# Self-attention over pixels on Trainium2: halves of the first image, the order of GpSimd's queue, and the last store

## The chip, the core and the metric

The kernel runs on one core of a Trainium2 (trn2) chip. The metric is the device time of one execution in microseconds (us); lower is better. Before the change the median of 3 runs is 163.97 us (163.97 to 164.14).

## The reference

For each of 4 images with 256 channels and 32x32 = 1024 pixels, in float32:

```python
q = einsum('oc,bcn->bon', Wq, xf) + bq      # 32 x 1024
k = einsum('oc,bcn->bon', Wk, xf) + bk      # 32 x 1024
v = einsum('oc,bcn->bon', Wv, xf) + bv      # 256 x 1024
attn = softmax(einsum('bqi,bqj->bij', q, k), axis=-1)
out = einsum('bcj,bij->bci', v, attn) + xf
```

## The kernel before, in words

**Numbers in two parts.** TensorE multiplies in the type fp32r. Each operand is cut into a high part (a cast) and a low part (the rest after the cast), and a product is three matmuls: high by high, high by low, low by high. So x, the weights, q, k, v and the exponentials all have a cast and a subtraction somewhere. `x_hi`, `x_lo`, `v_hi`, `v_lo`, `w_hi`, `w_lo` are these parts; the cast is mostly ScalarE's or VectorE's, the subtraction VectorE's or GpSimd's.

**Stages of an image.** (1) q and k are projected, 512 pixels at a time (`project_qk`, for image 0 `first_project_qk`). For images 1 to 3 their parts go by DMA into two stacks of 96 rows, `q_a` and `k_a` (helper `blocks`, L236), so that one matmul does the three products. (2) Score groups t = 0 to 7 of 128 query pixels by 1024 keys go to PSUM; VectorE takes the negative row maximum (L653), ScalarE the exponentials' sum (L492). Maximum and log of the sum are the shift of a row. (3) The shifts are turned into rows by a transpose (L692), split in two and sent by DMA as rows 96 and 97 of `q_b` (`send_rows`, L256). (4) The scores are made again, transposed, keys by queries, with the shift as two more rows of the contraction: the tiles `st` of L981, 16 an image, n = 16 b + 8 h + j, h being the half of the query pixels and j the block of 128 keys. ScalarE's exponential of a tile is then a finished softmax weight (L527 its high part, L530 in full); L400 or L720 make the low part. (5) `weigh_v` adds v times the weights into `acc`, three matmuls for each of two channel tiles (L994 twice, L1000 once). (6) VectorE adds x and the bias (`finish`), and SyncE stores.

**Image 0's first half is different.** Its sums aren't waited for: the shift of its 512 first query pixels is the maximum alone (`first_shifts`, `first_rows`, `put_first_rows`), and the result is divided afterwards. VectorE inverts the four sums of each partition (L667), SyncE writes them to a row in DRAM (`inv_row`, L312) and reads the row back on all partitions (`inv_all`, L316). At the end of that half VectorE multiplies `acc` by `inv_all` into `scaled` (L746), and GpSimd adds it to x (L467), to which ScalarE has added the bias (L506).

**The order of the work** is written out by hand. `turn(b)` has 16 steps; in step s TensorE makes the tile st of n + 2, weighs tile n, and then does the piece of the next image's front that `FRONT` (L44) gives to the step: score groups, q and k, v. Each other engine has a `turn` of its own, and waits on semaphores only. The order inside an engine's queue is thus what decides who is behind whom: GpSimd's loop (L451) comes at n = 8, 24 and 40 to the blocks of the next image's first half, to the shift rows of this image's second half, and to the blocks of the second half. `send_rows` waits until the rows are turned and, for b > 0, until the tiles that still read the old rows are done. The tile n = 8 (16 b + 8 in general) waits for `row_in[1]` of both rows, for `q_b` and for the exponential of tile n - 1.

```python
if j == 0:
    if b == 0 and h == 0:
        pe.wait_ge(row_put, 1)
    ...
    else:
        pe.wait_ge(row_in[h], rows_in(b, h))
    pe.wait_ge(qb_in[h], DMA * (b + 1))
```

**The start.** SyncE loads image 0 in two transfers, one for each tile of 128 channels (L275), then Wv (L276) and image 1 (L279). ScalarE loads the small weights (L473), which VectorE splits (L610, L612). x is cast and split in four pieces, `piece(i)`: channel tile i // 2, pixel half i % 2. TensorE goes through the same four (L861, L864, L866); the two halves of q and k are complete after pieces 2 and 3 (`qk_ready`). Then ScalarE makes k high (L542, both halves), the second quarter of q high (L548) and q in full for the second half (L553); VectorE makes the first quarter of q high (L754), q low (L634) and k low (L628); GpSimd copies q high (L372) behind the low part of Wv (L422). TensorE meanwhile does v tiles 0 and 1, then the score groups 0, 1, 2.

**The end.** The last image's second half lies in separate banks. `weigh_last_block` finishes channel tile 0, then the third and the fourth quarter of channel tile 1; `finish_last` (L729) evicts each quarter, and ScalarE's queue (L596) and SyncE's (L353) store them.

Of the kernel before, what the change touches and what calls it, by code (L numbers as in the profile page):

```python
# [6 lines left out]
def nonlocal_attention(nc, x, small, wv_t, out):  # L7
# [52 lines left out]
    with ctx:  # L60
# [3 lines left out]
        def sem(name):  # L64
            return ctx.enter_context(nc.semaphore(name))
# [36 lines left out]
        scaled = sb("scaled", [P, CT, HALF])  # L102
# [9 lines left out]
        x0_in = [sem(f"x0_in{c}") for c in range(CT)]  # L112
# [66 lines left out]
        x0_biased = sem("x0_biased")  # L179
        first_half_made = sem("first_half_made")  # L180
# [11 lines left out]
        def piece(i):  # L192

            return i // 2, cols(i % 2)
# [78 lines left out]
        def _(sp):  # L273
            for c in range(CT):
                sp.dma_start(x_sb[:, 0, c, :], x_v[0, :, c, :]).then_inc(x0_in[c], DMA)  # L275
# [35 lines left out]
            with nc.allow_non_contiguous_dma("512 numbers, long ahead of their use"):  # L311
                sp.dma_start(inv_row.rearrange("(t p) -> p t", p=P), inv[:, :]).then_inc(inv_put, DMA)  # L312
# [43 lines left out]
            sp.wait_ge(quarter_sent, DMA)  # L356

        @block.gpsimd
        def _(pool):
# [91 lines left out]
            for n in range(TH, TILES):  # L451
                b, more = n // PER, n // PER + 1 < BATCH
                if n % PER == JT:
                    if more:
                        second_blocks(b + 1, 0)
                    send_rows(pool, b, 1, (HI, LO) if more else (LO,))
                    if more:
                        second_blocks(b + 1, 1)
                split_w(n)
                if n == PER:  # L460

                    pool.wait_ge(w_split_pool, SPLIT_COUNT[n])
                    pool.wait_ge(st_ready, PER + 5)
                    pool.wait_ge(x0_biased, CT)
                    for c in range(CT):
                        pool.wait_ge(acc_read, c + 1)
                        nc.gpsimd.tensor_tensor(x_sb[:, 0, c, cols(0)], scaled[:, c, :], x_sb[:, 0, c, cols(0)],  # L467
                                                ALU.add).then_inc(first_half_made, 1)
                        pool.wait_ge(first_half_made, c + 1)

        @block.scalar
        def _(act):
            act.dma_start(small_sb[:, :], small).then_inc(small_in, DMA)  # L473
            act.preload_act_table_set("natural_log_exp_and_others")
            for i in range(4):
                c, part = piece(i)
                act.wait_ge(x0_in[c], DMA)
# [67 lines left out]
            def put_q_hi():  # L545

                act.wait_ge(q_lo_put, 1)
                nc.scalar.activation(q_a[2 * CQK:3 * CQK, Q_PARTS[1]], q_home(1),  # L548
# [10 lines left out]
            put_k_hi(0)  # L559
            put_k_hi(1)  # L560
            put_q_hi()
# [587 lines left out]
```

## Time and profile before

| | |
|---|---|
| median of 3 runs | 163.97 us (163.97 to 164.14) |
| profiled execution | 164.95 us |
| its span, first to last instruction | 163.2 us |
| mean granted TensorE clock | 0.998 of full speed |
| TensorE busy | 157.8 us (97%), 788 matmuls |
| VectorE busy | 133.3 us (82%) |
| ScalarE busy | 109.2 us (67%) |
| GpSimd busy | 57.3 us (35%) |
| DMA | 14.67 MB, mean 90 GB/s |

The profile is one execution; times within it are counted from its first instruction. PE is TensorE, DVE VectorE, ACT ScalarE, POOL GpSimd, SP SyncE; a q behind the name means its DMA queue. "x2" after an instruction means that two of them follow each other and are shown as one row with their time together. L981 is line 981 of the kernel. In brackets stands the idle time of the engine ahead of a row and who ended it. Instructions of one engine overlap a little at their ends, so two in a row take less than twice one.

### The profile page before, as it was taken

How to read it: one execution, taken by the hardware profiler on the slowest of the kernel's cores; microseconds unless marked ns; L12 is line 12 of the kernel's file. 1: busy time of each engine (PE TensorE's matmuls, PEld its weight loads, DVE VectorE, ACT ScalarE, POOL GpSimd, SP SyncE). 2: the span in 40 equal slices, each digit the busy share in tenths (PEclk: the TensorE clock that was granted, in tenths of full speed). 3: DMA queues.
4: the chain of work that ended last, by engine and by line, in shares of the span. 5: the costliest groups of instructions: out<-in, count | busy, mean ns of one | idle time of the engine just before them, and what ended most of it. 6: DMA issues, size and time to landing. Idle time of an engine off the chain costs nothing.

```text
span 163.2 us, 2451 instructions
## 1 busy us (share of the span) xinstructions
PE 157.8 (97%) x788; PEld 132.4 (81%) x788; DVE 133.3 (82%) x214; ACT 109.2 (67%) x200; POOL 57.3 (35%) x66
## 2 busy tenths in 40 slices
PE   7999999989999999999999999999999999999992
PEld 5677888778888898798888898789888898788882
DVE  1899998875988989996999989895989679846951
ACT  3679887958999647746999655745896655756400
POOL 4479945434243304733343300342433300124500
PEclk9999999999999999999999999999999999999999
DMA  4576796591002130246310230152220330003003
GB/s 157 190 296 177 229 46 27 151 290 51 25 30 60 37 129 2 57 108 209 129 48 18 83 129 2 33 135 78 96 84 1 96 129 0 0 5 129 0 0 129
DMA packets 8020, 14.67 MB, mean 90 GB/s; under 512 B 1872, under 2 KB 2312, under 8 KB 8008
## 3 DMA queue, kind: packets, MB, share of 16 engines
q1 hardware_dynamic: 7112, 13.52, 30.8%
q0 software_dynamic: 608, 0.80, 2.0%
q10 hardware_dynamic: 288, 0.20, 0.4%
q8 instruction: 6, 0.10, 0.4%
q14 instruction: 6, 0.05, 0.1%
HBM read 4.79 MB, written 4.20 MB: 55 GB/s over the span
## 4 chain that ended last, share of the span: by engine, by line
PE 90%; DMA 2%; ACT 2%; DVE 2%; issue 2%
PE acc L994 32%; PE acc L1000 16%; PE slot L834 11%; PE st L981 9%; PE slot L894 7%; PE slot L994 5%; DMA small_sb<-small 2%; PE slot L1000 2%; ACT dump L492 2%; PE slot L846 2%; PE slot L851 2%; PE slot L920 1%; DVE negmax L653 1%; PE slot L866 1%; DVE x_lo L618 0%
## 5 line engine op out<-in xcount | busy, mean ns | idle before, releaser
L400 POOL TENSOR_TENSOR w_lo<-w_full,w_hi 128x512 fp32r<-128x512 f32 x21 | 28.1, 1336 | 54.7 <-ACT w_full L530 31.0
L994 PE MATMUL acc<-w_hi,v_hi 128*128 128x512 f32 x112 | 44.3, 396 | 0.0
L994 PE MATMUL acc<-w_hi,v_lo 128*128 128x512 f32 x112 | 44.1, 394 | 0.0
L530 ACT ACTIVATE w_full<-st 128x512 f32<-128x512 f32 x62 | 36.8, 593 | 7.6 <-PE st L981 7.5
L492 ACT ACTIVATE dump<-slot,negmax 128x1024 f32<-128x1024 f32 x29 | 32.4, 1119 | 9.9 <-DVE negmax L653 9.5
L653 DVE TENSOR_REDUCE negmax<-slot 128x1 f32<-128x1024 f32 x29 | 35.2, 1216 | 3.8 <-PE slot L894 3.8
L1000 PE MATMUL acc<-w_lo,v_hi 128*128 128x512 f32 x112 | 37.4, 396 | 0.0
L720 DVE TENSOR_TENSOR w_lo<-w_full,w_hi 128x512 fp32r<-128x512 f32 x43 | 31.6, 740 | 3.3
L981 PE MATMUL st<-q_b,k_b 98*128 98x512 f32 x62 | 24.6, 399 | 0.9 <-issue 0.8
L994 PEld LDWEIGHTS acc<-w_hi,v_hi 128*128 128x128 f32 x112 | 21.1, 189 | 5.0 <-issue 0.3
L994 PEld LDWEIGHTS acc<-w_hi,v_lo 128*128 128x128 f32 x112 | 21.2, 189 | 4.8
L1000 PEld LDWEIGHTS acc<-w_lo,v_hi 128*128 128x128 f32 x112 | 21.0, 188 | 4.8
L711 DVE CAST w_hi<-w_full 128x512 fp32r<-128x512 f32 x40 | 18.0, 453 | 3.1 <-ACT w_full L530 1.5
L527 ACT ACTIVATE w_hi<-st 128x512 fp32r<-128x512 f32 x24 | 14.3, 595 | 7.1 <-PE st L981 7.1
L834 PE MATMUL slot<-wv_hi,x_hi 128*128 128x256 f32 x62 | 17.4, 281 | 0.4 <-ACT dump L492 0.4
L834 PE MATMUL slot<-wv_lo,x_hi 128*128 128x256 f32 x62 | 17.4, 280 | 0.0
L834 PE MATMUL slot<-wv_hi,x_lo 128*128 128x256 f32 x62 | 17.3, 280 | 0.0
L894 PE MATMUL slot<-k_a,q_a 96*128 96x512 f32 x48 | 15.2, 397 | 0.0
L519 ACT ACTIVATE v_hi<-slot 128x512 fp32r<-128x512 f32 x12 | 7.2, 599 | 11.8 <-PE slot L834 11.8
L701 DVE TENSOR_TENSOR v_lo<-slot,v_hi 128x512 fp32r<-128x512 f32 x16 | 11.0, 690 | 4.4 <-ACT v_hi L519 4.2
L894 PEld LDWEIGHTS slot<-k_a,q_a 96*128 96x128 f32 x48 | 13.0, 310 | 1.1
L981 PEld LDWEIGHTS st<-q_b,k_b 98*128 98x128 f32 x62 | 11.6, 188 | 2.4 <-issue 1.0
(101 smaller groups left out, 214.9 us busy)
## 6 DMA issues: line engine op xcount, KB each, us to landing
out<-x_sb SPq DMA_DIRECT2D x7, 512.0 KB, 2.8
x_sb<-x SPq DMA_DIRECT2D x3, 1024.0 KB, 6.3
k_b<-k_a SPq DMA_DIRECT2D x8, 192.0 KB, 2.6
q_b<-q_a SPq DMA_DIRECT2D x8, 192.0 KB, 2.6
x_sb<-x SPq DMA_DIRECT2D x2, 512.0 KB, 4.2
k_a<-qk_parts SPq DMA_DIRECT2D x12, 64.0 KB, 2.3
q_a<-qk_parts SPq DMA_DIRECT2D x12, 64.0 KB, 2.3
k_a<-qk_parts POOLq DMA_DIRECT2D x6, 64.0 KB, 2.6
```

The lines of the kernel that those rows point to most:

```text
L400: nc.gpsimd.tensor_tensor(w_lo[:, r, :], w_full[:, r, :], w_hi[:, r, :].bitcast(fp32), ALU.subtract).then_inc(w_split_pool, 1)
L492: nc.scalar.activation(dump[:, t % 2, :], s_home(b, t), ACT.Exp, bias=negmax[:, t:t + 1], accum_out=rowsum[:, t:t + 1]).then_inc(rowsum_re ...
L527: nc.scalar.activation(w_hi[:, r, :], st_home(n), ACT.Exp).then_inc(w_cut_act, 1)
L530: nc.scalar.activation(w_full[:, r, :], st_home(n), ACT.Exp).then_inc(exp_done, 1)
L653: nc.vector.tensor_reduce(out=negmax[:, t:t + 1], in_=s_home(b, t), op=ALU.max, axis=AX.X, negate=True).then_inc(negmax_ready, 1)
L711: nc.vector.tensor_copy(w_hi[:, r, :], w_full[:, r, :]).then_inc(w_cut_dve, 1)
L720: nc.vector.tensor_tensor(w_lo[:, r, :], w_full[:, r, :], w_hi[:, r, :].bitcast(fp32), ALU.subtract).then_inc(w_split_dve, 1)
L834: last = nc.tensor.matmul(dst, lhs, rhs, start=(i == 0), stop=(i == len(terms) - 1))
L894: last = nc.tensor.matmul(s_home(b, t)[:, cols(h)], pixels(b, t), k_a[0:K_A, cols(h)], start=True, stop=True)
L981: nc.tensor.matmul(st_home(n), k_b[0:K_B, j * P:(j + 1) * P], q_b[0:K_B, cols(h)], start=True, stop=True).then_inc(st_ready, 1)
L994: nc.tensor.matmul(dst, v[:, b % 2, j, c * P:(c + 1) * P], w_hi[:, n % RING, part], start=(j == 0 and v is v_hi), stop=False)
L1000: return nc.tensor.matmul(dst, v_hi[:, b % 2, j, c * P:(c + 1) * P], w_lo[:, n % RING, part], start=False, stop=(j == JT - 1))
```

## The change

1. Image 0 is loaded in two transfers by pixel halves (each with both channel tiles, rows of 2 KB and not 4 KB), and cast, split and projected in that order.
2. ScalarE makes the first quarter of q high too, between the two halves of k high; VectorE begins with k low.
3. TensorE makes score group 0 ahead of v tile 1.
4. `inv_row` keeps the order in which the sums lie in SBUF, so a partition writes 16 bytes in one piece; the readers undo the order.
5. VectorE copies `acc` of image 0's first half and doesn't multiply; GpSimd multiplies it by `inv_all` after step n = 16 and adds it to x at n = 24, ahead of its subtraction for tile 24.
6. GpSimd sends the shift rows ahead of the blocks of the next image's first half.
7. The last quarter is evicted in two pieces of 128 columns, stored by SyncE and by ScalarE's queue.

```diff
-                sp.dma_start(x_sb[:, 0, c, :], x_v[0, :, c, :]).then_inc(x0_in[c], DMA)
+                sp.dma_start(x_sb[:, 0, :, cols(h)], x_v[0, :, :, cols(h)]).then_inc(x0_in[h], DMA)
...
         def piece(i):
-            return i // 2, cols(i % 2)
+            return i % CT, cols(i // CT)
...
+        LAST_PIECES = ((slice(0, QUARTER),), (slice(QUARTER, QUARTER + P), slice(QUARTER + P, HALF)))
...
-                sp.dma_start(inv_row.rearrange("(t p) -> p t", p=P), inv[:, :]).then_inc(inv_put, DMA)
+            sp.dma_start(inv_row.rearrange("(p t) -> p t", p=P), inv[:, :]).then_inc(inv_put, DMA)
...
             sp.wait_ge(acc_read, 4 * BATCH + 1)
-            sp.dma_start(out_v[BATCH - 1, :, 1, quarter(3)], x_sb[:, BATCH - 1, 1, quarter(3)]).then_inc(out_sent[1], DMA)
+            sp.dma_start(out_v[BATCH - 1, :, 1, N - QUARTER:N - P], x_sb[:, BATCH - 1, 1, N - QUARTER:N - P]).then_inc(out_sent[1], DMA)
...
                 if n % PER == JT:
-                    if more:
-                        second_blocks(b + 1, 0)
                     send_rows(pool, b, 1, (HI, LO) if more else (LO,))
                     if more:
-                        second_blocks(b + 1, 1)
+                        for h in range(2):
+                            second_blocks(b + 1, h)
+                if n == PER + JT:
+                    pool.wait_ge(st_ready, n + 1)
+                    pool.wait_ge(x0_biased, CT)
+                    for c in range(CT):
+                        nc.gpsimd.tensor_tensor(x_sb[:, 0, c, cols(0)], undivided[:, c, :], x_sb[:, 0, c, cols(0)],
+                                                ALU.add).then_inc(first_half_made, 1)
+                    pool.wait_ge(first_half_made, CT)
                 split_w(n)
                 if n == PER:
                     pool.wait_ge(w_split_pool, SPLIT_COUNT[n])
-                    pool.wait_ge(st_ready, PER + 5)
-                    pool.wait_ge(x0_biased, CT)
+                    pool.wait_ge(inv_in, DMA)
                     for c in range(CT):
                         pool.wait_ge(acc_read, c + 1)
-                        nc.gpsimd.tensor_tensor(x_sb[:, 0, c, cols(0)], scaled[:, c, :], x_sb[:, 0, c, cols(0)],
-                                                ALU.add).then_inc(first_half_made, 1)
-                        pool.wait_ge(first_half_made, c + 1)
+                        pool.wait_ge(w_split_dve, SPLIT_COUNT[PER + AHEAD + c])
+                        nc.gpsimd.tensor_tensor(undivided[:, c, :].rearrange("p (t q) -> p t q", t=TH),
+                                                undivided[:, c, :].rearrange("p (t q) -> p t q", t=TH),
+                                                inv_all[:, :].rearrange("p (q t) -> p t q", t=TH),
+                                                ALU.mult).then_inc(first_half_divided, 1)
+                    pool.wait_ge(first_half_divided, CT)
...
             put_k_hi(0)
+            put_q_hi(0)
             put_k_hi(1)
-            put_q_hi()
+            put_q_hi(1)
             put_q2_full()
...
+            act.wait_ge(acc_read, 4 * BATCH + 2)
+            act.dma_start(out_v[BATCH - 1, :, 1, N - P:N], x_sb[:, BATCH - 1, 1, N - P:N]).then_inc(quarter_sent, DMA)
...
                 if (b, h) == (0, 0):
-                    dve.wait_ge(inv_in, DMA)
-                    nc.vector.tensor_tensor(scaled[:, c, :], acc[:, c, :], inv_all[:, :],
-                                            ALU.mult).then_inc(acc_read, 1)
+                    nc.vector.tensor_copy(undivided[:, c, :], acc[:, c, :]).then_inc(acc_read, 1)
                     return
...
-            dve.wait_ge(qk_ready, 1)
-            nc.vector.tensor_scalar(out=q_a[2 * CQK:3 * CQK, Q_PARTS[0]], in0=q_home(0),
-                                    scalar1=bias[2 * CQK:3 * CQK, 0:1], scalar2=None,
-                                    op0=ALU.add).then_inc(q_hi_put, 1)
+            put_k_lo(0)
             put_q_lo(0)
-            put_k_lo(0)
             put_k_lo(1)
             put_q_lo(1)
...
-                dst = qk_home(0, i % 2)
+                dst = qk_home(0, i // CT)
...
             v_tile(0, 0)
+            first_scores(0)
             v_tile(0, 1)
-            first_scores(0)
             first_scores(1)
             first_scores(2)
```

## Rows read from the trace of the kernel before

**Rows 1.** Stretch 36.6 to 160.3 us: busy of each engine (instructions), TensorE clock, DMA.
```profile
36.60:160.30 123.70, 123.69 (x612) 105.22 (x612) 102.93 (x165) 82.08 (x152) 35.29 (x34) 1.00 0.21 65
```

**Rows 2.** Chain of waits, start: start us, us, what.
```profile
0.76 3.94 DMA small_sb<-small
...
5.47 0.71 DVE x_lo L618
...
8.57 0.23 PE slot L866
```

**Rows 3.** TensorE in order of time, 35 to 75 us: start us, us, instruction.
```profile
35.50 0.28 PE L834 MATMUL slot<-wv_hi,x_lo 128*128 128x256 f32 x1
36.57 0.47 PE L981 MATMUL st<-q_b,k_b 98*128 98x512 f32 x1 [0.79 <-issue]
...
38.29 0.63 PE L894 MATMUL slot<-k_a,q_a 96*128 96x512 f32 x2
...
73.95 0.28 PE L834 MATMUL slot<-wv_hi,x_lo 128*128 128x256 f32 x1
74.07 0.40 PE L981 MATMUL st<-q_b,k_b 98*128 98x512 f32 x1
```

**Rows 4.** VectorE, GpSimd and SyncE's queue in order of time, 30 to 35 us.
```profile
30.24 0.41 DVE L692 STREAM_TRANSPOSE shift_rows<-shift_parts 128x128 f32<-128x128 f32 x1
...
30.82 0.65 POOL L237 DMA_DIRECT2D k_a<-qk_parts  x1 [2.45 <-ACT qk_parts L485]
...
31.96 1.16 POOL L262 DMA_DIRECT2D q_b<-shift_rows  x2
...
34.53 0.59 SPq L237 DMA_DIRECT2D k_a<-qk_parts  x1
```

**Rows 5.** DMA issues: KB each, us to landing; all, then from 17, then from 31.9.
```profile
x_sb<-x SPq DMA_DIRECT2D x3, 1024.0 KB, 6.3
...
out<-x_sb SPq DMA_DIRECT2D x1, 128.0 KB, 1.9
...
q_b<-shift_rows POOLq DMA_DIRECT2D x7, 2.0 KB, 2.4
...
x_sb<-x SPq DMA_DIRECT2D x1, 1024.0 KB, 13.6
inv_row<-inv SPq DMA_DIRECT2D x1, 2.0 KB, 10.5
...
q_b<-shift_rows POOLq DMA_DIRECT2D x2, 2.0 KB, 4.0
```

**Rows 6.** DMA queues, 3.2 to 3.7 us: packets, MB, share of 16 engines.
```profile
q1 hardware_dynamic: 42, 0.17, 83.5%
q10 hardware_dynamic: 43, 0.02, 15.0%
```

**Rows 7.** ScalarE, VectorE and TensorE in order of time, 4 to 15 us.
```profile
4.51 1.15 ACT L478 ACTIVATE x_hi<-x_sb 128x512 fp32r<-128x512 f32 x2 [2.04 <-DMA x_sb<-x]
...
8.21 1.31 ACT L542 ACTIVATE k_a<-slot,small_sb 64x512 fp32r<-64x512 f32 x2 [0.70 <-PE slot L866]
...
9.18 1.40 DVE L628 SCALAR_TENSOR_TENSOR k_a<-slot,small_sb,k_a 32x512 fp32r<-32x512 f32 x2
...
13.68 0.73 PE L920 MATMUL acc<-k_a,q_a 96*128 96x512 f32 x2
...
14.57 1.21 DVE L653 TENSOR_REDUCE negmax<-acc 128x1 f32<-128x1024 f32 x1
```

**Rows 8.** GpSimd, then TensorE in order of time, 63 to 79 us.
```profile
63.35 2.78 POOL L467 TENSOR_TENSOR x_sb<-scaled,x_sb 128x512 f32<-128x512 f32 x2 [7.92 <-PE st L981]
...
78.96 0.39 PE L1000 MATMUL acc<-w_lo,v_hi 128*128 128x512 f32 x1
```

**Rows 9.** VectorE in order of time, the last evictions.
```profile
157.48 0.75 DVE L750 SCALAR_TENSOR_TENSOR x_sb<-slot,small_sb,x_sb 128x512 f32<-128x512 f32 x1 [0.94 <-PE slot L1000]
...
160.33 0.48 DVE L729 SCALAR_TENSOR_TENSOR x_sb<-slot,small_sb,x_sb 128x256 f32<-128x256 f32 x1 [0.94 <-PE slot L1000]
```

More of the change, by code:

```diff
@@ L110, in nonlocal_attention @@
         slot = [ctx.enter_context(nc.psum_tensor(f"slot{i}", [P, N], fp32)) for i in range(2)]
-        x0_in = [sem(f"x0_in{c}") for c in range(CT)]
+        x0_in = [sem(f"x0_in{h}") for h in range(2)]
         x1_in = sem("x1_in")
@@ L179, in nonlocal_attention @@
         x0_biased = sem("x0_biased")
+        first_half_divided = sem("first_half_divided")
         first_half_made = sem("first_half_made")
@@ L310, in _ @@
             sp.wait_ge(inv_ready, 1)
-            with nc.allow_non_contiguous_dma("512 numbers, long ahead of their use"):
-                sp.dma_start(inv_row.rearrange("(t p) -> p t", p=P), inv[:, :]).then_inc(inv_put, DMA)
+            sp.dma_start(inv_row.rearrange("(p t) -> p t", p=P), inv[:, :]).then_inc(inv_put, DMA)
             sp.wait_ge(x_in, DMA)
@@ L453, in _ @@
                 if n % PER == JT:
-                    if more:
-                        second_blocks(b + 1, 0)
                     send_rows(pool, b, 1, (HI, LO) if more else (LO,))
                     if more:
-                        second_blocks(b + 1, 1)
+                        for h in range(2):
+                            second_blocks(b + 1, h)
[6 more added lines that the diff above has]
+                    pool.wait_ge(first_half_made, CT)
                 split_w(n)
@@ L476, in _ @@
                 c, part = piece(i)
-                act.wait_ge(x0_in[c], DMA)
+                act.wait_ge(x0_in[i // CT], DMA)
                 nc.scalar.activation(x_hi[:, 0, c, part], x_sb[:, 0, c, part], ACT.Copy).then_inc(x0_cut, 1)
@@ L723, in finish_last @@
             def finish_last(i):
-                part = slice(HALF + i * QUARTER, HALF + (i + 1) * QUARTER)
                 if i == 0:
@@ L728, in finish_last @@
                     dve.wait_ge(av_done, TILES)
-                nc.vector.scalar_tensor_tensor(
-                    out=x_sb[:, BATCH - 1, 1, part], in0=last_half(1)[i][1],
-                    scalar=bv_sb[:, 1:2], in1=x_sb[:, BATCH - 1, 1, part],
-                    op0=ALU.add, op1=ALU.add).then_inc(acc_read, 1)
+                for px in LAST_PIECES[i]:
+                    part = slice(HALF + px.start, HALF + px.stop)
+                    nc.vector.scalar_tensor_tensor(
+                        out=x_sb[:, BATCH - 1, 1, part],
+                        in0=last_half(1)[i][1][:, px.start - i * QUARTER:px.stop - i * QUARTER],
+                        scalar=bv_sb[:, 1:2], in1=x_sb[:, BATCH - 1, 1, part],
+                        op0=ALU.add, op1=ALU.add).then_inc(acc_read, 1)
             def finish(b, h, c):
```

12 lines of the change are left out of this document (6 added, 6 removed).

## The prediction

> **What bounds the kernel now.** I read the stretches first, then the chain of waits, then each engine in order of time. From 36.6 to 160.3 us TensorE is busy 123.69 of 123.70 us at the full granted clock, the upper of its two levels (2.4 GHz) [rows 1]. In that stretch no work on another engine can shorten the run; it can only lengthen it, by being late for a matmul. Three places are left: the start, one hole near 36 us, and the last eviction and store.
>
> The start's chain runs from the small weights, which land 3.94 us after their issue, over VectorE's first split of x at 5.47 and TensorE's projection, whose last matmul begins at 8.57 [rows 2], to the splits of q and k, the first row maxima and the exponentials. The hole [rows 3]: image 1's v projection starts its last matmul at 35.50, and the next instruction, the score tile n = 8, starts at 36.57, 0.79 us of that idle with no releaser named. At the same place of image 2 the two stand at 73.95 and 74.07. The distance is 1.07 us against 0.12, and the tile behind the wait takes 0.47 us and not 0.40. So the hole costs 0.95 + 0.07 = 1.02 us.
>
> Who is late? That tile waits for the two transfers of shift rows. Their numbers are ready at 30.24 + 0.41 = 30.65, but GpSimd issues two q, k blocks first (from 30.82) and the two rows only from 31.96, for 1.16 us together, the second so at about 32.54 [rows 4]. They need 4.0 us to land, where 2.4 is the median of such rows [rows 5]: 32.54 + 4.0 = 36.54, and the tile starts at 36.57. They are slow because the queues are full: x of image 3, issued beside inv_row, took 13.6 us, where 6.3 is the median of three such images, and inv_row, 2 KB in pieces of 4 bytes, took 10.5 us [rows 5].
>
> **The change, part by part.**
>
> *The hole.* Two edits meet. inv_row is written in 128 pieces of 16 bytes, no longer 512 of 4. If the cost goes by piece, 10.5 us becomes 2 + 8.5/4, about 4 us (2 for a landing that waits for nothing, as the last store's 1.9 [rows 5]); image 3 and the broadcast of inv behind it land before 30 us, and the blocks and rows meet idle queues. And GpSimd sends the rows ahead of its blocks, at 30.7 and 31.3. Landing in 2.4 us, the second is there at 33.7, 1.9 us before TensorE would ask at 35.62. If the queues stay full, 4.0 us give 35.3, and as what is issued sooner waits longer for the same queue I leave 0.4 us of wait. Term -1.02; ends -0.6 and -1.02. I take the upper end, since image 2 landed twice as fast without inv_row beside it. The Trainium skill, page "DMA: Bandwidth & Descriptors", section "Specifications", says that below 512 B the engine does a read-modify-write; pieces of 16 bytes remain below, so that would leave a cost for each of the 128, and the same term.
>
> Moved past: GpSimd's four blocks end their issue when they did, as only their order with the rows changes and the last two wait for the second half's cut. Of SP's own blocks the last one that image 1's first scores need is issued at 34.53 [rows 4]. With the start's gain (below) that is 34.15, landed with 2.4 us at 36.55; the scores, now at 38.29 [rows 3], would come at 38.29 - 1.40 = 36.89. The cover is 0.3 us; price 0, at worst 0.4.
>
> *The start.* Pieces 0 and 1 are now the two channel tiles of the first 512 pixels. The first half of q and k is complete three matmuls of 0.23 us (0.70) sooner, the second half no sooner, at 8.80 [rows 2]. ScalarE casts k high 0, q high 0, k high 1. Its two k casts now run from 8.21 for 1.31 us, to 9.52 [rows 7]: k high 1 is bound by the second half's 8.80 and still ends there, and q high 0 fits in front of it. VectorE loses q high 0. Its two k low splits end at 9.18 + 1.40 = 10.58 now [rows 7]; with k low 0 done long before, k low 1 takes 0.74 us (half of the 1.40 and a start of its own) from 9.55, to 10.29. So the first maximum comes 0.29 us sooner. But score group 0 now stands ahead of v tile 1 (6 matmuls, 0.70 us), which then delays groups 1 to 3: group 3 starts at about 13.75 (13.68 now), takes 0.73, so the fourth maximum, now at 14.57, starts at 14.4 [rows 7]. Of 0.29 us 0.18 are left at the shift rows, for which TensorE waits next.
>
> Beyond this, x arrives in rows of 2 KB. From 3.2 to 3.7 us 42 rows of q1 (x, 4 KB) went beside 43 of q10 (the small weights), one for one. A row of q1 takes 0.835 x 16 x 0.5 / 42 = 0.159 us of an engine, one of q10 0.028 us [rows 6]. The eight small rows of an engine so take 8 x 0.187 = 1.5 us; beside x rows of half the size 8 x 0.108 = 0.9, 0.6 us less. Not all of it counts: x's first cast starts at 4.51 [rows 7] and takes some 0.6, so the first split, at 5.47 now, can gain 0.34 at most. For twice the rows of x I allow 0.14 back. So 0.20 more. Term for the start: -(0.18 + 0.20) = -0.38; ends 0 and -0.55.
>
> The Trainium skill, page "DMA: Bandwidth & Descriptors", section "Queues, rings and completion order", says that an engine drains a packet of about 9 to 17 descriptors from one queue before it turns to the next. The trace's one for one does not look like that; by the rule x's row size would not matter here, and this term would be -0.18.
>
> *The first half of image 0.* VectorE copies acc and no longer multiplies it, the same 128x512 read of PSUM, at a place where TensorE is never late: 0. GpSimd takes over the multiplication, two operations more, in the gap before 63.35 where it sat idle for 7.92 us [rows 8]: 0. Its two additions move to behind the tile n = 24, which starts at 74.07 [rows 3], and hold back GpSimd's w_lo of n = 24: tile done 74.47, additions 2.78 us as now, 77.3, then w_lo (as one addition, 1.39) 78.7. TensorE uses it at 78.96 [rows 8]. Cover 0.3 us; price 0, at worst 0.15 if each of the three ran 0.14 slower. SP's store of that half waits for the additions; what is queued behind it waits for image 1's eviction at the same place anyway: 0.
>
> *The end.* The last eviction of 256 columns becomes two of 128. 512 columns took 0.75 us and 256 took 0.48 [rows 9], so 128 take about 0.35; started 0.25 apart, they end 0.12 later than now. The second store moves 64 KB where one moved 128 KB in 1.9 us [rows 5]; I allow 0.07 for the smaller size. Term +0.05; ends -0.1 and +0.15.
>
> **Sum.** -1.02 - 0.38 + 0.05 = -1.35 us. The profiled execution took 164.95 us (span 163.2, 1.75 around it) and would take 163.60. The median, 163.97, lies 0.98 below the profiled one; I carry the difference over: 162.62. About 0.2% (0.33 us) is what a measurement of this kernel can tell from no change.
>
> **The rivals.**
> 1. *The small weights land as before*, by the page's packets or because halves of x cost what is won. The start gives 0.18, the sum is -1.15: 162.8 us. For it: no row prices x in 2 KB rows at this moment. Chance 0.20.
> 2. *The queues stay full*: inv_row costs by the transfer, not by the piece, and only the new order helps. -0.6 - 0.38 + 0.05: 163.0 us. For it: no 16-byte piece is in the trace. Chance 0.10.
> 3. *A cover of 0.3 us fails*, that of w_lo 24 or of the last k block, by 0.3 to 0.4: 163.0 us. The Trainium skill, page "SBUF — State Buffer", section "Who interferes with whom", says that a VectorE instruction with two SBUF inputs contends with GpSimd's reads. The 1.39 us an addition is a row beside a busy VectorE. Chance 0.13.
> 4. *The change doesn't do what it is for*: the hole has another cause and stays. -0.38 + 0.05: 163.64 us, the edge of no change. Against it: 36.54 and 36.57 agree. Chance 0.07.
> 5. *Slower*: GpSimd's multiplication reads inv with a stride of four numbers, which no row shows, and the shift rows of image 1's second half stand behind it in its queue. They must be issued by 71 us to be in at 74; the multiplications begin near 61.3, so it decides from some 4.5 us each. At 6 us each the rows land near 77 and TensorE waits 2.9 us: 165.5 us. Against: that is over four times an addition. Chance 0.04.
>
> **Numbers.** The forecast keeps 0.46. Range 162.1 to 163.5: below, the start's 0.55 and a shorter tail, and 0.2 for the carrying over; above, rivals 1 to 3 with the upper end of the tail and one of the covers. Faster by over 0.2%: forecast and rivals 1 to 3, 0.89, less 0.02 for several at once; within 0.2%: rival 4 and near misses, 0.08; slower 0.05.
>
> **What the next profile would show.** Right: no idle time ahead of the tile behind image 1's v projection; inv_row lands in 3 to 5 us and image 3 in 6 to 8; the small weights are used near 4.2; k low 1 ends 0.3 to 0.5 sooner; the additions run from 74.5 less the gain, and w_lo 24 is in time. Wrong: a new TensorE gap at image 1's first scores or at its n = 8, or multiplications of over 3 us on GpSimd, or 4.7 us again for the small weights.

## The result: no gain, and the profile after

In 14 executions each, the changed kernel took 164.22 us (median; 164.03 to 164.43) and the kernel before 163.94 us (163.79 to 164.29). The ratio is 1.0015, with a 95% interval of 1.0008 to 1.0022: slower by 0.15%, inside the 0.2% that the prediction called no change. 162.6 us was forecast, with a range of 162.1 to 163.5. The profiled execution took 164.22 us (span 162.4). Below, "before" and "after" without an article mean the profiled executions of the two kernels, and the name of an experiment its profiled execution where a time within it is given.

The stretch from the end of the old hole to the last evictions, as in [rows 1]: TensorE is busy at the full granted clock, and the hole in front of it is gone (second fence, in order of time; the answer to [rows 3]).

```profile
36.10:159.60 123.50, 123.48 (x613) 105.06 (x611) 103.67 (x166) 82.58 (x153) 38.01 (x36) 1.00 0.21 67
```

```profile
35.90 0.28 PE L847 MATMUL slot<-wv_hi,x_lo 128*128 128x256 f32 x1
36.02 0.40 PE L994 MATMUL st<-q_b,k_b 98*128 98x512 f32 x1
```

The two starts lie 0.12 us apart, where there were 1.07. But the last matmul of the v projection, which started at 35.50, now starts at 35.90. The transfers [rows 5] did what the forecast said, and more; the DMA issues from 0 to 60 us (KB each, us to landing):

```profile
x_sb<-x SPq DMA_DIRECT2D x2, 512.0 KB, 4.7
...
q_b<-shift_rows POOLq DMA_DIRECT2D x2, 2.0 KB, 1.7
...
inv_row<-inv SPq DMA_DIRECT2D x1, 2.0 KB, 2.1
```

inv_row lands in 2.1 us and not 10.5, the shift rows in 1.7 and not 4.0. The 0.4 us by which the v projection is late are lost at the start. ScalarE, then VectorE, then GpSimd in order of time (the answer to [rows 7]):

```profile
4.98 1.15 ACT L490 ACTIVATE x_hi<-x_sb 128x512 fp32r<-128x512 f32 x2 [2.50 <-DMA x_sb<-x]
6.40 1.15 ACT L490 ACTIVATE x_hi<-x_sb 128x512 fp32r<-128x512 f32 x2 [0.27 <-DMA x_sb<-x]
7.45 0.61 ACT L570 ACTIVATE wv_hi<-wv 128x512 fp32r<-128x512 f32 x1
7.97 0.67 ACT L554 ACTIVATE k_a<-slot,small_sb 64x512 fp32r<-64x512 f32 x1
8.67 0.47 ACT L561 ACTIVATE q_a<-slot,small_sb 32x256 fp32r<-32x256 f32 x1
9.16 0.68 ACT L554 ACTIVATE k_a<-slot,small_sb 64x512 fp32r<-64x512 f32 x1
```

```profile
3.79 0.29 DVE L626 CAST wqk_hi<-small_sb 128x256 fp32r<-128x256 f32 x1 [2.51 <-DMA small_sb<-small]
...
8.68 0.74 DVE L644 SCALAR_TENSOR_TENSOR k_a<-slot,small_sb,k_a 32x512 fp32r<-32x512 f32 x1 [0.32 <-ACT k_a L554]
9.45 0.48 DVE L650 SCALAR_TENSOR_TENSOR q_a<-slot,small_sb,q_a 32x256 fp32r<-32x256 f32 x1
9.96 0.74 DVE L644 SCALAR_TENSOR_TENSOR k_a<-slot,small_sb,k_a 32x512 fp32r<-32x512 f32 x1
...
14.81 1.23 DVE L669 TENSOR_REDUCE negmax<-acc 128x1 f32<-128x1024 f32 x1
16.15 0.38 DVE L676 CAST shift_parts<-negmax 128x4 fp32r<-128x4 f32 x1
```

```profile
15.89 0.61 POOL L408 CAST x_hi<-x_sb 128x512 fp32r<-128x512 f32 x1
16.58 1.31 POOL L412 TENSOR_TENSOR x_lo<-x_sb,x_hi 128x512 fp32r<-128x512 f32 x1
```

The first cast of x starts 0.47 us later than before (4.51), k low 1 ends at 10.70 (10.58), and the fourth maximum starts at 14.81 (14.57). VectorE's cast of the shifts takes 0.38 us and ends with GpSimd's cast beside it: 15.89 + 0.61 = 16.50, 16.15 + 0.38 = 16.53. Before, VectorE and GpSimd:

```profile
15.89 0.20 DVE L660 CAST shift_parts<-negmax 128x4 fp32r<-128x4 f32 x1
16.13 0.17 DVE L662 TENSOR_TENSOR shift_parts<-negmax,shift_parts 128x4 fp32r<-128x4 f32 x1
...
20.72 2.35 DVE L653 TENSOR_REDUCE negmax<-slot 128x1 f32<-128x1024 f32 x2
```

```profile
15.45 0.61 POOL L406 CAST x_hi<-x_sb 128x512 fp32r<-128x512 f32 x1
```

The image's first half and the end, the answers to [rows 8] (GpSimd) and [rows 9] (VectorE):

```profile
60.74 1.54 POOL L477 TENSOR_TENSOR undivided<-undivided,inv_all 128x512 f32<-128x512 f32 x1 [6.00 <-DVE w_lo L736]
63.86 1.55 POOL L477 TENSOR_TENSOR undivided<-undivided,inv_all 128x512 f32<-128x512 f32 x1 [1.58 <-DVE w_lo L736]
...
73.87 2.54 POOL L466 TENSOR_TENSOR x_sb<-undivided,x_sb 128x512 f32<-128x512 f32 x2 [2.73 <-PE st L994]
76.49 2.54 POOL L402 TENSOR_TENSOR w_lo<-w_full,w_hi 128x512 fp32r<-128x512 f32 x2
```

```profile
159.62 0.61 DVE L747 SCALAR_TENSOR_TENSOR x_sb<-slot,small_sb,x_sb 128x128 f32<-128x128 f32 x2 [0.94 <-PE slot L1013]
```

### The profile page after: what moved, and what is told of

Same layout as the page of the kernel before. It is cut to its first block, busy times and chain, and to the rows that moved or that the text cites. A ratio compares the mean times of both kernels' runs of the same rounds, so it can differ in the third digit from the quotient of the medians.

```text
span 162.4 us, 2456 instructions
## 1 busy us (share of the span) xinstructions
PE 157.1 (97%) x788; PEld 131.9 (81%) x788; DVE 133.8 (82%) x214; ACT 109.6 (67%) x201; POOL 59.2 (36%) x68
## 4 chain that ended last, share of the span: by engine, by line
PE 90%; DMA 3%; ACT 2%; DVE 1%; issue 1%; SPq 0%; DVEq 0%
PE acc L1007 32%; PE acc L1013 16%; PE slot L847 13%; PE st L994 9%; PE slot L907 7%; PE slot L1007 5%; DMA x_sb<-x 3%; PE slot L1013 2%; PE slot L859 2%; PE slot L864 2%; PE slot L933 1%; DVE k_a L644 1%; ACT dump L504 1%; ACT x_hi L490 1%; ACT k_a L554 0%
## 5 line engine op out<-in xcount | busy, mean ns | idle before, releaser
L736 DVE TENSOR_TENSOR w_lo<-w_full,w_hi 128x512 fp32r<-128x512 f32 x43 | 30.7, 719 | 3.3
L727 DVE CAST w_hi<-w_full 128x512 fp32r<-128x512 f32 x40 | 19.5, 490 | 3.0 <-ACT w_full L542 1.4
L265 POOL DMA_DIRECT2D q_b<-shift_rows x7 | 4.2, 602 | 29.5 <-DVE shift_rows L708 27.0
```

Of the source, the lines that this page charges most:

```text
L727: nc.vector.tensor_copy(w_hi[:, r, :], w_full[:, r, :]).then_inc(w_cut_dve, 1)
L736: nc.vector.tensor_tensor(w_lo[:, r, :], w_full[:, r, :], w_hi[:, r, :].bitcast(fp32), ALU.subtract).then_inc(w_split_dve, 1)
```

## The experiments

Each kernel was timed in five rounds beside the kernel before on the same chip. "Ratio" is to that kernel; its own median stands in the last column, since it moved from chip to chip. A median is that of 12 or 13 executions, but of 6 for rest_alone and rest_beside and of 5 for four_back.

| kernel | median us (range) | ratio, 95% | before there |
|---|---|---|---|
| before_again | 164.19 (163.84 to 165.09) | 0.9989, 0.9972 to 1.0007 | 164.45 |
| start_alone | 164.92 (164.28 to 165.31) | 1.0024, 1.0007 to 1.0041 | 164.45 |
| rest_alone | 163.82 (163.73 to 164.10) | 0.9962, 0.9943 to 0.9981 | 164.45 |
| load_alone | 164.61 (164.09 to 165.78) | 1.0014, 0.9991 to 1.0036 | 164.45 |
| whole | 164.32 (164.15 to 164.49) | 1.0002, 0.9990 to 1.0014 | 164.28 |
| order_back | 164.23 (164.05 to 164.40) | 0.9998, 0.9987 to 1.0009 | 164.28 |
| inv16_alone | 164.52 (164.40 to 164.87) | 1.0018, 1.0005 to 1.0030 | 164.28 |
| rows_first_alone | 164.01 (163.88 to 164.74) | 0.9989, 0.9975 to 1.0003 | 164.28 |
| tiles_4k | 164.22 (164.11 to 164.33) | 0.9987, 0.9973 to 1.0001 | 164.32 |
| rows_2k | 164.29 (164.03 to 164.95) | 1.0001, 0.9987 to 1.0016 | 164.32 |
| rest_again | 163.89 (163.75 to 164.18) | 0.9971, 0.9956 to 0.9987 | 164.32 |
| rest_old_end | 163.92 (163.82 to 164.09) | 0.9975, 0.9964 to 0.9986 | 164.32 |
| four_loads | 164.21 (163.75 to 164.39) | 0.9982, 0.9967 to 0.9997 | 164.40 |
| four_back | 163.89 (163.70 to 163.93) | 0.9966, 0.9954 to 0.9978 | 164.40 |
| rest_beside | 163.81 (163.73 to 164.12) | 0.9965, 0.9952 to 0.9978 | 164.40 |
| four_clear | 164.67 (164.18 to 164.99) | 1.0008, 0.9995 to 1.0022 | 164.43 |
| whole_clear | 164.91 (164.82 to 166.71) | 1.0022, 1.0009 to 1.0035 | 164.43 |
| rest_clear | 164.67 (164.52 to 164.92) | 1.0010, 0.9995 to 1.0026 | 164.43 |

### The change cut in two: before_again, start_alone, rest_alone, load_alone

before_again is the kernel before with nothing changed, for a second look at its hole. start_alone is that kernel with items 1 to 3 of the change (the loads, ScalarE's q, the score group), rest_alone the changed kernel without them, so items 4 to 7. load_alone is the kernel before with item 1 alone:

```diff
-            for c in range(CT):
-                sp.dma_start(x_sb[:, 0, c, :], x_v[0, :, c, :]).then_inc(x0_in[c], DMA)
+            for h in range(2):
+                sp.dma_start(x_sb[:, 0, :, cols(h)], x_v[0, :, :, cols(h)]).then_inc(x0_in[h], DMA)
...
-            return i // 2, cols(i % 2)
+            return i % CT, cols(i // CT)
...
-                dst = qk_home(0, i % 2)
+                dst = qk_home(0, i // CT)
```

Expected of before_again:

> The kernel before, unchanged, for another profiled execution. Theory A (the hole near 36 us belonged to one execution, not to the kernel): span near 162.2 us, no idle time ahead of the score tile behind image 1's v projection, time within 0.1% of the kernel before. Theory B (the hole is in every execution and the change filled it, but lost as much elsewhere): span near 163.2 us with 0.7 us or more of idle time at that place.

Expected of start_alone:

> The kernel before with the start's edits alone (x of image 0 by halves, ScalarE makes q high's first quarter, score group 0 ahead of v tile 1). Theory A: all of the loss is here and a little more, since the last store gains: +0.3 to +0.5 us against the kernel before. Theory B (the loss comes from GpSimd's new work or its order): 0 to +0.1 us, or the 0.38 us less that were forecast.

Expected of rest_alone:

> The changed kernel with the start as in the kernel before; it keeps inv_row by 16 bytes, the rows ahead of the blocks, GpSimd's multiplication and the last store in two pieces. Theory A (no hole in most executions, the last store gains a little): -0.05 to -0.2 us against the kernel before. Theory B (GpSimd's part loses): +0.2 us or more. If the hole were in every execution of the kernel before: -1.0 us.

Expected of load_alone:

> The kernel before with only the load, the cast and the projection of image 0 by halves; q high's first quarter stays with VectorE, the score groups keep their place. Theory A1 (x lands about 0.4 us later because the small weights' rows now pass ahead of x, and this is what costs): x's first cast near 5.0 us and not 4.5, +0.2 to +0.4 us. Theory A2 (the order of score group 0 and v tile 1 is what costs): 0 us or a gain.

The two parts pull against each other: items 4 to 7 win (0.9962), items 1 to 3 lose (1.0024). Item 1 alone is unclear in its median (1.0014, with 1 inside the interval). And before_again showed what no single trace could. TensorE in order of time in its profile:

```profile
35.48 0.28 PE L834 MATMUL slot<-wv_hi,x_lo 128*128 128x256 f32 x1
35.81 0.47 PE L981 MATMUL st<-q_b,k_b 98*128 98x512 f32 x1
```

In the same kernel the two starts lie 0.33 us apart here, where [rows 3] has 1.07 and a matmul without a hole 0.12. In start_alone and load_alone, which keep the old rest, it is 36.95 - 35.86 = 1.09 and 36.29 - 35.91 = 0.38: a hole of another length each time. These three kernels are spread over 1.0 to 1.7 us, rest_alone over 0.37. The hole explains the profiled times to 0.05 us. Counted as the prediction counts it, it cost 1.02 us in before, 0.28 in before_again and 0.69 in rows_2k (below), whose transfers were those of the kernel before. Without it 163.93, 163.88 and 163.89 us are left of the 164.95, 164.16 and 164.58.

### Which edit closes the hole: inv16_alone, rows_first_alone

inv16_alone is the kernel before with inv_row in pieces of 16 bytes; VectorE's multiplication (L746) undoes the order. rows_first_alone is the kernel before with item 6 alone.

```diff
...
-                sp.dma_start(inv_row.rearrange("(t p) -> p t", p=P), inv[:, :]).then_inc(inv_put, DMA)
+            sp.dma_start(inv_row.rearrange("(p t) -> p t", p=P), inv[:, :]).then_inc(inv_put, DMA)
...
```

```diff
-                    if more:
-                        second_blocks(b + 1, 0)
                     send_rows(pool, b, 1, (HI, LO) if more else (LO,))
                     if more:
-                        second_blocks(b + 1, 1)
+                        for h in range(2):
+                            second_blocks(b + 1, h)
```

> The kernel before with inv_row in pieces of 16 bytes alone; VectorE's multiplication reads inv_all with a stride. Theory A: inv_row lands in about 2 us, the hole is gone, the spread of the times is under 0.5 us, the median 163.8 to 163.95 us. Theory D (the order of GpSimd's queue fills the hole, not the queues' load): the hole stays at 0.3 us or more.

> The kernel before with the shift rows ahead of the blocks on GpSimd alone. Theory A (the queues are full until image 3 and the broadcast have landed, whatever is issued first): the rows are issued 1.1 us sooner and land 0.3 to 1.1 us sooner, the hole shrinks but the spread stays near 1 us. Theory D: the hole is gone and so is the spread.

Either closes it in its profile. inv16_alone, TensorE, and the transfer of image 3 from 15 to 40 us; then the same two of rows_first_alone:

```profile
35.88 0.28 PE L835 MATMUL slot<-wv_hi,x_lo 128*128 128x256 f32 x1
35.99 0.40 PE L982 MATMUL st<-q_b,k_b 98*128 98x512 f32 x1
...
x_sb<-x SPq DMA_DIRECT2D x1, 1024.0 KB, 5.3
```

```profile
35.63 0.28 PE L833 MATMUL slot<-wv_hi,x_lo 128*128 128x256 f32 x1
35.75 0.40 PE L980 MATMUL st<-q_b,k_b 98*128 98x512 f32 x1
...
x_sb<-x SPq DMA_DIRECT2D x1, 1024.0 KB, 12.8
```

With 16-byte pieces image 3 lands in 5.3 us; with 4-byte pieces it still takes 12.8, and the rows, sent first, are in time all the same, but not by much. They need 3.1 us here, the second from about 32.2 on, so they are in at 35.3 for a tile at 35.75; the 4.0 us of [rows 5] would be too late (an estimate from these rows). The times say so too: rows_first_alone is spread over 0.86 us, with 3 of its 12 executions at 164.25, 164.54 and 164.74, inv16_alone over 0.47. So the order by itself closes the hole in most executions, as far as the times show, and not in all. inv16_alone isn't faster for it, because VectorE's strided multiplication costs more than the hole. VectorE, first there and then in before_again:

```profile
39.44 2.06 DVE L745 TENSOR_TENSOR scaled<-acc,inv_all 128x512 f32<-128x512 f32 x2
```

```profile
39.33 1.28 DVE L746 TENSOR_TENSOR scaled<-acc,inv_all 128x512 f32<-128x512 f32 x2
```

TensorE's score tile behind the two starts at 42.84 and not 42.21, where it was 0.08 late ahead of them: 0.55 us. GpSimd's strided multiplications (1.54 and 1.55 us above) stand where nobody waits for them, so item 5 is what makes item 4 pay.

### Why the start loses: whole, order_back, tiles_4k, four_loads, four_back

whole is the changed kernel again, a second look with its start in the same series. The other four are the changed kernel with one thing each: order_back puts v tile 1 ahead of score group 0 again; tiles_4k loads by channel tile again, in rows of 4 KB, and keeps the order of the pieces; four_loads loads image 0 in four transfers of 256 KB in the order of the pieces; four_back is four_loads with order_back's edit.

```diff
-            for h in range(2):
-                sp.dma_start(x_sb[:, 0, :, cols(h)], x_v[0, :, :, cols(h)]).then_inc(x0_in[h], DMA)
+            for i in range(4):
+                c, part = piece(i)
+                sp.dma_start(x_sb[:, 0, c, part], x_v[0, :, c, part]).then_inc(x0_in[i], DMA)
...
```

> The changed kernel, unchanged, on the chip on which the kernel before is timed beside it. Theory A (the hole near 36 us is there in every execution but of changing length, 0.3 to 1.1 us, since inv_row's slow write lands at changing times): the times lie within 0.5 us of each other, where those of the kernel before spread over 1 us or more; the median is 0.3 to 0.6 us above the kernel without the start's edits (163.82 us), so at 164.1 to 164.4.

> The changed kernel with v tile 1 again ahead of score group 0. Theory A (x's late landing costs 0.2 us and more, the order of the score group the rest): 0.1 to 0.2 us below the whole change, and the fourth maximum starts 1.13 us after the third. Theory C (the order is neutral, the loss is all x's landing): the same time as the whole change.

> The changed kernel, projected by halves, but image 0 loaded by channel tile in rows of 4 KB as before, so that piece 1 waits for the second transfer. Theory E: x's first cast is back at 4.5 us and the last at 6.9 us; since piece 1 now starts with the second transfer, TensorE ends its projections near 8.8 us, as in the whole change: 164.1 to 164.4 us, 0.3 us or more above the kernel without the start's edits.

> The changed kernel with image 0 in four transfers of 256 KB, a quarter for each piece, in the order of the pieces; the rows stay at 2 KB. Theory G (only the landing of the halves is late; the new order of the start is worth the 0.2 to 0.3 us that were forecast once x is there in time): first cast at 4.5 us or sooner, first maximum 0.2 us or more sooner than in the kernel before, 0.3 to 0.6 us less than the whole change: 163.7 to 164.0 us. Theory H (the new order is worth nothing, since VectorE's three steps and ScalarE's three casts follow each other without cover and v tile 1 delays the groups behind): the first cast is in time, the time stays at 164.1 us or above.

> The same with v tile 1 ahead of score group 0 again. Theory G: 0.1 us below the one with the new place, as for the whole change (164.32 against 164.23 us), so 163.6 to 163.9 us. Theory H: 164.0 us or above.

First the load. x's first cast starts at 4.46 to 4.66 us in every kernel that loads by channel tile, tiles_4k (4.59) among them, and at 4.97 to 5.28 in every one that loads by halves. The queues from 3.2 to 3.7 us (packets, MB, share of 16 engines); start_alone, then whole:

```profile
q1 hardware_dynamic: 53, 0.11, 77.9%
q10 hardware_dynamic: 50, 0.03, 18.9%
```

```profile
q1 hardware_dynamic: 70, 0.14, 90.8%
q10 hardware_dynamic: 11, 0.00, 2.2%
```

A row of 2 KB takes 0.779 x 8 / 53 = 0.118 us or 0.908 x 8 / 70 = 0.104 us of an engine here, and not half of the 0.159 us of a row of 4 KB [rows 6]. By these two the first 512 KB, 256 such rows, need 1.66 to 1.89 us of 16 engines, where 128 of the old ones took 1.27: 0.4 to 0.6 us more (an estimate). The small weights do land sooner in whole and after, 3.0 us after their issue, and are used at 3.8, as the forecast had it, but x is late by then and nothing is won. In start_alone, order_back and tiles_4k they need 3.9 to 4.0. So in some executions the weights' rows pass x's one for one, in others not. rows_2k, the kernel before with each row of x written as two, was meant to price the row by itself, but its rows went out joined again (as many packets on q1 as before). The same 2 KB rows, 4 KB apart too, took less in the kernels with four transfers: in the same half microsecond 80 of them went by in four_back at 89.2%, which is 0.089 us each, and 96 in four_clear at 91.4%, 0.076. So neither the size nor the distance alone makes them dear; what does stays open.

Nor is late x the whole loss. tiles_4k has x's first cast in time and is no faster than whole: 164.22 us, 0.33 above rest_again beside it. Its piece 1 needs the second channel tile and so waits for the second transfer; its last cast of x ends at 5.90 + 1.67 = 7.57, that of after at 6.40 + 1.15 = 7.55.

> The kernel before with image 0 still loaded by channel tile, but each row of 4 KB written as two pieces of 2 KB. Theory E (a row of 2 KB costs the queue more than half a row of 4 KB, at the start of the stream above all): twice the rows of x in the queue's count, x's first cast near 4.9 us and not 4.5, the time 0.2 to 0.4 us above the kernel before. Theory F (the late landing has to do with the two halves lying 4 KB apart, not with the size of a row): x's first cast near 4.5 us.

Then the order of the work. v tile 1's place changes little in the halves kernel (order_back, 164.23 against 164.32). Between four_loads and four_back lie 0.32 us (164.21 and 163.89), but that this is the order isn't shown. The two load x alike, and yet TensorE's last projection matmul starts 0.77 us apart in their profiles; four_loads, then four_back:

```profile
8.54 0.39 PE L880 MATMUL slot<-x_lo,wqk_hi 128*128 128x512 f32 x1
```

```profile
7.77 0.48 PE L880 MATMUL slot<-x_lo,wqk_hi 128*128 128x512 f32 x1
```

In four_clear, which loads as four_back does and has its order, it is 8.37. So the landing of four transfers moves from execution to execution, and four_back's median is that of five. Its profile has everything of the forecast's start: the first cast at 3.85, the last projection matmul at 7.77 and not 8.41, the fourth maximum at 14.20. Still the last matmul of image 1's v projection starts at 35.41 us, in rest_beside at 35.55, in the kernel before at 35.50. In VectorE's and GpSimd's order of time, four_back:

```profile
14.20 1.22 DVE L670 TENSOR_REDUCE negmax<-acc 128x1 f32<-128x1024 f32 x1
15.52 0.48 DVE L677 CAST shift_parts<-negmax 128x4 fp32r<-128x4 f32 x1
16.04 0.17 DVE L679 TENSOR_TENSOR shift_parts<-negmax,shift_parts 128x4 fp32r<-128x4 f32 x1
...
20.63 2.35 DVE L670 TENSOR_REDUCE negmax<-slot 128x1 f32<-128x1024 f32 x2
```

```profile
15.37 0.61 POOL L409 CAST x_hi<-x_sb 128x512 fp32r<-128x512 f32 x1
```

The cast of 128x4 numbers begins 0.37 us earlier than in the kernel before (15.89) and ends 0.09 earlier, at 16.00, 0.02 after GpSimd's 15.98. In before it ended at 16.09 (GpSimd 16.06), in start_alone at 16.47 (16.44), in after at 16.53 (16.50), in whole at 16.57 (16.54). That is a gate nobody wrote: GpSimd's second cast of image 1, whose place follows from ScalarE's q in full for the second half, over GpSimd's copies and splits of q. In before that q ends at 10.58, in after at 11.00, and GpSimd's work behind it is 0.42 to 0.44 us later. The Trainium skill, page "SBUF — State Buffer", section "Who interferes with whom", says that a VectorE copy or cast in its two-port mode and a GpSimd instruction exclude each other for the whole instruction. The common ends agree with it; the last three kernels try it. Common ends alone prove little: in load_alone the maxima are so late (the fourth at 15.02) that the cast takes 0.17 us, and it still ends 0.04 after GpSimd's.

What the end of this cast decides can be read from VectorE. From the subtraction behind it VectorE works without a pause up to image 1's first row maximum, which starts 4.59 us later in before (20.72 - 16.13) and in four_back (20.63 - 16.04), and 4.59 to 4.60 later in all 17 profiles in which GpSimd's queue is not edited as below. The last matmul of image 1's v projection starts 19.37 to 19.43 us after the cast's end in the same 17. four_back's first score tiles do start 0.29 us before those of before (17.39 and 17.68), but at 23.84 and 23.93 only 0.09 of it is left. So TensorE gains at 35 us what the cast of the shifts gains at 16, and no more.

### The gate taken away: four_clear, whole_clear, rest_clear

four_back, the changed kernel, and rest_alone, each with this edit of GpSimd's queue:

```diff
+            pool.wait_ge(shift_ready, 1)
             cut_x1(1)
             split_x1(1)
             pool.wait_ge(x1_split, 2)
-            pool.wait_ge(shift_ready, 1)
             cut_x1(2)
             split_x1(2)
             pool.wait_ge(x1_split, 3)
-            cut_x1(3)
-            pool.wait_ge(x1_cut, 4)
             split_w(1)
+            cut_x1(3)
+            pool.wait_ge(x1_cut, 4)
```

> The kernel four_back (image 0 in four transfers, v tile 1 ahead of score group 0, everything else as in the change), and in GpSimd's queue its second cast of image 1 (L408) waits until the first shifts are split (shift_ready), while the fourth cast goes behind the subtraction for tile 1. So no cast of GpSimd runs beside VectorE's cast of the shifts. Theory 'the shift cast is held by GpSimd's cast': in four_back the cast of the shifts took 0.48 us and ended with GpSimd's cast at 15.98; here it takes 0.20 or less and starts as soon as the fourth maximum is made, TensorE's first weighted matmuls come 0.2 to 0.35 us sooner, and the median is 163.55 to 163.7. Rival 'the maxima and the transposition set the pace, the common end with GpSimd's cast is chance': within 0.1 us of four_back, 163.8 to 164.0. Third way: GpSimd is now so late with w_lo 1 or x_lo of image 1 that TensorE waits at 20 to 24 us: over 164.0.

> The changed kernel with the same edit of GpSimd's queue. Its shift cast took 0.38 us and ended with GpSimd's cast at 16.5. Held by GpSimd: the cast takes 0.20 or less, the median falls by 0.15 to 0.3, to 163.9 to 164.1. Chance: stays at 164.2 to 164.3.

> The change with the start as before, and the same edit of GpSimd's queue. There the shift cast starts late anyway (15.9 us) and took 0.20 us. Both theories: 0 to 0.1 us less than 163.85; held by GpSimd: the cast takes under 0.20 us.

All three are slower by 0.6 to 0.9 us than the kernel they come from, and the hold on the cast is shown all the same. VectorE, four_clear:

```profile
14.69 1.22 DVE L669 TENSOR_REDUCE negmax<-acc 128x1 f32<-128x1024 f32 x1
16.01 0.17 DVE L676 CAST shift_parts<-negmax 128x4 fp32r<-128x4 f32 x1
16.22 0.17 DVE L678 TENSOR_TENSOR shift_parts<-negmax,shift_parts 128x4 fp32r<-128x4 f32 x1
...
19.61 1.49 DVE L736 TENSOR_TENSOR w_lo<-w_full,w_hi 128x512 fp32r<-128x512 f32 x1
```

The cast takes 0.17 us, in the other two as well. In this execution the maxima were 0.49 us later than in four_back, the shifts only 0.18: 0.31 us came back, which is 0.48 - 0.17. But GpSimd's subtraction of x is now 1.1 us later and meets VectorE's first subtraction for a weight. GpSimd, then TensorE, four_clear:

```profile
19.26 1.29 POOL L413 TENSOR_TENSOR x_lo<-x_sb,x_hi 128x512 fp32r<-128x512 f32 x1
```

```profile
21.16 0.73 PE L1013 MATMUL acc<-w_lo,v_hi 128*128 128x512 f32 x2 [0.42 <-DVE w_lo L736]
```

VectorE's subtraction took 0.68 us in four_back and takes 1.49 here: it stands until GpSimd is done at 20.55, and then needs its 0.55. In all three the first maximum of image 1 now comes 5.40 to 5.41 us after the subtraction of the shifts and not 4.59, and the v projection 20.2 us after the cast and not 19.4: the 0.8 us that TensorE is later by. So the third way on record came true in its place and its price, though with VectorE's subtraction and not GpSimd's; for whole_clear and rest_clear, where a gain or nothing was expected, it wasn't thought of. A version that takes the first collision away without the second wasn't tried, so what the hold costs in the time isn't measured; 0.31 us in four_back and about 0.2 in after (0.38 - 0.17) are what it takes from the cast.

### The last store: rest_again, rest_old_end, rest_beside

rest_again and rest_beside are rest_alone once more; rest_old_end evicts and stores the last quarter in one piece.

> The changed kernel with the start of the kernel before, once more, for an interval. Theory A: 163.8 to 163.95 us with a spread under 0.5 us, 0.3 to 0.6 us below the median of the kernel before on this chip and 0.4 to 0.5 us below the whole change.

> The same with the last quarter evicted and stored in one piece, as in the kernel before. Theory A (the two pieces gain, since 64 KB land 0.2 to 0.3 us sooner and the second eviction costs 0.13 us): 0.05 to 0.15 us above the kernel with two pieces. The forecast's term: 0.05 us below it.

> The changed kernel with the start of the kernel before, beside the two with four transfers, so that the three share their comparison: 163.8 to 163.95 us. Theory G: it is beaten by the one with v tile 1 ahead, by 0.05 to 0.3 us. Theory H: it stays the best.

163.89 against 163.92, with intervals that overlap: no difference is shown. From the start of the last matmul to the end of the span pass 3.1 us with them and 3.2 in the kernel before.

## Why the prediction was wrong

It forecast -1.35 us from the median of the kernel before. Items 4 to 7 gave -0.4 to -0.6 us in three comparisons, items 1 to 3 cost 0.4 to 0.5 (start_alone 0.47 above its before, 0.39 by the ratio; whole 0.4 to 0.5 above the kernels without them). The sum is about nothing. Two steps failed: the hole was priced from one execution (1), and the start was credited with 0.38 us where it lost 0.4 (3 to 5).

1. **The carrying over** failed first: "The median, 163.97, lies 0.98 below the profiled one; I carry the difference over". The difference wasn't around the span, it was mostly the hole. The profiled execution stood 0.98 us above the median, and its hole cost 1.02 us where in another profile of the kernel it cost 0.28. The carried difference and the term are thus the same microsecond, taken off twice. So the term of -1.02 was mis-sized: right for the execution that was read (the changed kernel's profile has 0.95 us less there), some 0.4 to 0.6 beside the medians of 164.3 to 164.45. On the first chip, where before's median was 163.94, less can have been there (an estimate: 0.1, from the 163.85 of the kernels without a hole and with the old start). With the start's 0.4 that makes +0.3; +0.28 was measured. On the other chips it was 164.28 to 164.45, while the changed kernel stayed at 164.22 and 164.32.
2. **The hole's mechanism was right**: inv_row's pieces, the slow rows, the order. Even the landing (about 4 us forecast, 2.1 measured) erred to the safe side. The rows were issued later than forecast, in rows_first_alone at 31.43 and not 30.7, 0.6 us after they are turned. The pieces alone would have done; the order alone does in most executions.
3. **"beside x rows of half the size 8 x 0.108 = 0.9"** failed, and the 0.14 for twice the rows with it. A 2 KB row took 0.104 to 0.118 us there, not 0.080, and x's first cast came 0.5 us late. The order of the pieces gains nothing either when the rows stay at 4 KB (tiles_4k). The rule weighed there, that an engine drains a packet of one queue before it turns (the Trainium skill, "DMA: Bandwidth & Descriptors", "Queues, rings and completion order"), would have x's row size not matter: by it 162.8. start_alone's 53 beside 50 rows doesn't look like it, as [rows 6] didn't; whole's 70 beside 11 might, and neither gave a gain.
4. **"q high 0 fits in front of it"** failed, and with it k low 1's end at 10.29; it came at 10.70. k high 1 was to end at 9.52 as before and ended at 9.84. The old start had 0.70 us of idle ScalarE ahead of its k casts [rows 7]; with x late that is gone, and from 6.40 on ScalarE does two casts of x, Wv's, k high 0, q high 0 and k high 1 without a pause. VectorE's k low 0, q low 0 and k low 1 follow one another directly from 8.68, and q low 0, which the step forgot, costs another 0.1.
5. **"at the shift rows, for which TensorE waits next"** failed too: the step from the maxima on was taken one for one. What counts is when VectorE's cast of the shifts ends, since VectorE has no pause behind it. It ended 0.44 us later in after: the maxima gave 0.24 to 0.26 of it, and 0.18 is the longer cast, held by GpSimd's. That one hangs on ScalarE's q, which late x moves back as well as item 2: in load_alone, with item 1 alone, the cast ends at 16.51, as late as in after. How much item 2 costs by itself wasn't tried.
6. **The end** was forecast at +0.05, and no difference was measured. **The covers** held: the additions began at 73.87, the subtraction for tile 24 at 76.49, and TensorE used it at 78.27 without waiting.

Of the rivals, the first is partly what happened (the start's gain given back, but by more than was won), the second did not (full queues), nor the third and the fifth: a strided multiplication took 1.55 us where 4.5 would have hurt. The fourth, that the hole stays, was wrong in kind, yet its number, 163.64 and "the edge of no change", came nearest. That the start could lose was no rival at all: its end was 0, with no row behind that bound. No rival asked whether the term of -1.02 and the carried 0.98 were the same time.

## What to carry to other kernels

Before a gap in one profile is priced, hold that execution against the median: what stands 1 us above it has its own holes, and a second profile of the same kernel costs less than a wrong sum. Where a gain is passed from engine to engine, look also at what runs beside each link on another engine: two ends that agree to 0.04 us while one of the durations varies are a likely wait, to be tried by moving one of them. And follow the engine that has no pause: here VectorE, and not TensorE's next wait. Loading in the order of use wasn't free here. Of all the kernels rest_alone (items 4 to 7 alone) is the one to keep: 163.81 to 163.89 in three series, beside 164.32 to 164.45 for the kernel before.

## What was unexpected in the hardware

512 pieces of 4 bytes took 9.2 to 10.5 us, 128 of 16 bytes 1.9 to 2.6 us, about what the last store of 128 KB took (1.9 [rows 5]). The 1 MB load of image 3 went from 12.7 to 13.6 us down to 4.8 to 5.8, in the profiles where it stands in a row of its own.

In whole_clear's profile the first projections ran at the half rate. TensorE in order of time, and the stretch 7 to 10 us (columns as in [rows 1]):

```profile
7.46 0.63 PE L873 MATMUL slot<-x_hi,wqk_hi 128*128 128x512 f32 x1
7.89 0.63 PE L876 MATMUL slot<-x_hi,wqk_lo 128*128 128x512 f32 x1
```

```profile
7.00:10.00 3.00, 3.00 (x8) 2.31 (x7) 1.76 (x4) 2.28 (x5) 1.28 (x1) 1.00 0.51 141
```

From 6.61 to 10.03 they start 0.43 us apart and not 0.23, although the granted clock is shown as 1.00 there. TensorE had stood idle for 0.54 us ahead of them; in after it stood for 0.69, and 0.23 us apart was reached from the fourth matmul on. In rest_alone and inv16_alone the first three distances were 0.42 to 0.57 us too, and their projections ended 0.3 us late, which the times of these two profiles (164.10 and 164.87, the highest of their kernels) contain. whole_clear's took 166.71 us, 1.8 above the median of its kernel. Why it fell on this one is open.
